# Differential cross-attention and a routed feed-forward layer on one core: a step of sixteen chunks laid out as eight slots of two chunks, with the side work of every engine in a new order

## The reference

```python
n = layernorm(x)
q, k, v = n @ Wq.T, ctx @ Wk.T, ctx @ Wv.T          # q, k: 32 sub-heads of 8; v: 16 heads of 16
att = softmax(q_j @ k_j.T / sqrt(8))                # 128 x 128 for each of 32 sub-heads
att = att[even] - lam * att[odd]                    # 16 heads
x = x + att @ v
h = layernorm(x)
shared = silu(h @ ws_gate) * (h @ ws_up) @ ws_down
w, e = top_k(sigmoid(h @ gate_w.T), 2); w = 2.5 * w / sum(w)
x = x + shared + sum_k w_k * (silu(h @ w_gate[e_k]) * (h @ w_up[e_k])) @ w_down[e_k]
```

## Time and profile before

| | |
|---|---|
| median of 3 runs | 2256.83 us (2256.3 to 2265.62) |
| the profiled execution, its own time | 2249.22 us |
| its span in the trace | 2247.5 us |
| PE busy | 2021.7 us, 90% of the span |
| DVE, ACT, POOL busy | 71%, 63%, 64% |
| mean granted TensorE clock | 0.972 of full speed |
| DMA | 432.05 MB, mean 192 GB/s |

### The profile page before, as it was taken

How to read it: one execution, slowest core, us unless ns; L and a number is a source line. 1 busy time by engine, 2 the same in 40 slices (tenths; PEclk the granted TensorE clock), 3 DMA queues, 4 the chain that set the end, 5 groups by cost and what they waited for, 6 DMA issues and landing times.

```text
span 2247.5 us, 76469 instructions
## 1 busy us (share of the span) xinstructions
PE 2021.7 (90%) x20840; PEld 1405.2 (63%) x20840; DVE 1584.5 (71%) x4623; ACT 1426.2 (63%) x3511; POOL 1446.2 (64%) x2183
## 2 busy tenths in 40 slices
PE   4999999999999999999999999999977988889996
PEld 3666665566656566656656566666546877768775
DVE  3777777777777777778777777778765655546554
ACT  2777777777777777777776777777763444434443
POOL 4466777767677676767676767767664555545554
PEclk8899999999999999999999999999987999999999
DMA  5997777777777777777777777878846777667774
GB/s 133 222 225 192 187 195 190 178 189 184 191 190 184 186 194 185 185 183 182 191 193 178 184 188 190 194 181 216 228 173 180 223 214 214 199 178 220 220 223 127
DMA packets 616921, 432.05 MB, mean 192 GB/s; under 512 B 447811, under 2 KB 562634, under 8 KB 616400
## 3 DMA queue, kind: packets, MB, share of 16 engines
q1 hardware_dynamic: 556528, 319.91, 58.3%
q0 software_dynamic: 32256, 84.47, 11.8%
q10 hardware_dynamic: 28000, 26.03, 3.8%
HBM read 234.59 MB, written 197.72 MB: 192 GB/s over the span
## 4 chain that ended last, share of the span: by engine, by line
PE 67%; DVE 15%; issue 10%; ACT 3%; DMA 2%; SPq 1%; POOL 1%; DVEq 1%; another core or an unknown queue 1%; ACTq 0%; POOLq 0%
PE mx_ps L494 11%; PE o_ps L527 7%; DVE mx L982 6%; PE ms_ps L778 5%; PE o_ps L538 5%; PE ms_ps L555 5%; PE mx_ps L557 4%; PE mx_ps L555 4%; PE ms_ps L576 4%; PE st_ps L756 3%; PE mx_ps L556 3%; PE ms_ps L583 3%; PE st_ps L487 3%; PE ms_ps L556 3%; PE ms_ps L557 2%
## 5 line engine op out<-in xcount | busy, mean ns | idle before, releaser
L982 DVE TENSOR_REDUCE mx<-mx_ps 128x4 f32<-128x512 f32 x1024 | 686.3, 685 | 300.4 <-PE mx_ps L494 294.2
L826 ACT ACTIVATE prob<-st_ps 128x512 f32<-128x512 f32 x1024 | 604.5, 598 | 357.8 <-PE st_ps L487 353.5
L494 PE MATMUL mx_ps<-stacks 48*128 48x128 bf16 x4096 | 396.7, 221 | 67.6 <-DVE mx L982 33.8
L487 PE MATMUL st_ps<-stacks 50*128 50x128 bf16 x4096 | 394.9, 220 | 0.0
L494 PEld LDWEIGHTS mx_ps<-stacks 48*128 48x128 bf16 x4096 | 230.9, 95 | 228.6 <-issue 105.9
L527 PE MATMUL o_ps<-prob,v_sb 128*32 128x256 f32 x4096 | 331.6, 396 | 0.8 <-ACT prob L826 0.4
L1344 POOL DMA_INDIRECT rows_dram<-rowt,posi x256 | 253.7, 991 | 67.6 <-issue 64.3
L555 PE MATMUL ms_ps<-e_lo 128*128 128x256 f32 x768 | 264.7, 345 | 18.1 <-issue 11.1
L923 ACT ACTIVATE rows_T<-st_ps 128x256 fp32r<-128x256 f32 x288 | 111.7, 388 | 192.2 <-PE st_ps L756 137.3
L487 PEld LDWEIGHTS st_ps<-stacks 50*128 50x128 bf16 x4096 | 229.8, 95 | 2.5 <-issue 1.5
L1413 POOL DMA_INDIRECT sums_dram<-stacks x144 | 141.7, 984 | 130.4 <-DVE stacks L1220 70.2
(11 more groups left out here) (155 smaller groups left out, 4694.4 us busy)
## 6 DMA issues: line engine op xcount, KB each, us to landing
stack_dram<-w_dn_sb SPq DMA_DIRECT2D x768, 128.0 KB
stacks<-stack_dram SPq DMA_DIRECT2D x512, 192.0 KB
stacks<-rows_dram SPq DMA_DIRECT2D x288, 130.0 KB
w_dn_sb<-in_x SPq DMA_DIRECT2D x64, 256.0 KB
w_dn_sb<-in_ctxT SPq DMA_DIRECT2D x64, 256.0 KB
x_res<-in_x SPq DMA_DIRECT2D x64, 256.0 KB
stacks<-sums_dram SPq DMA_DIRECT2D x78, 128.0 KB
stacks<-base_dram SPq DMA_DIRECT2D x76, 128.0 KB
```

The source lines that it names most:

```text
L487: return pe.matmul(st_ps[k % 2][:, i * P:(i + 1) * P], k_st[p][64 * h:64 * h + KROWS, u, j, :], q_st[p][64 * h:64 * h + KROWS, u, j, :], s ...
L494: return pe.matmul(mx_ps[k % 2][:, i * P:(i + 1) * P], q_st[p][64 * h:64 * h + ROWS, u, j, :], k_st[p][64 * h:64 * h + ROWS, u, j, :], sta ...
L826: nc.scalar.activation(prob[k % 4][:, :], st_ps[k % 2][:, :], ACT.Exp, scale=float(HALF) ** -0.5).then_inc(a_exp, 1)
L982: v.tensor_reduce(mx[:, u, c * CHUNK:(c + 1) * CHUNK], mx_ps[k % 2][:, :].rearrange("p (c n) -> p c n", c=CHUNK), AX.X, ALU.max).then_inc( ...
```

## The change

What it does, part by part:

- **Slots.** The loop over 16 chunks becomes one over 8 slots (`NSL`), each of two chunks. `st_ps` and `mx_ps` become one tensor over two banks each; one exponential and one reduction read 1024 columns. TensorE now waits, before it writes slot n, for the exponential and the reduction of slot n-1, since both banks are read by one instruction. `attend` of a slot comes a slot later. Semaphore counts follow.
- **Side jobs.** The two halves of `value` and of each projection are issued together; all side jobs have new slots; `gate_up` signals each half.
- **VectorE.** `shared_gate`/`shared_up` and `low`/`shared_add` stand ahead of the slot's reduction; `indices` is split off `best_two`. The arithmetic of `places` works on a copy `rank` in SBUF, which ScalarE makes by one more instruction of 128 columns a step, and TensorE's `clear` waits for this copy.
- **GpSimd.** The scatters of pair `r` move one step later (`r3 = it-3`); `split` of the queries moves to the next step, behind two scatters and a residual.
- **SyncE.** The twelve parts are issued together, after `put_max(it, 1)`; the four loads for the next step's first half stand together, then `put_max(b, 0)`.
- **The ends.** Two more steps are written out ahead of the loop, and the experts' weight splits at the stage's end keep nearly their places.

```diff
-            def both(it, b, k, do_c, do_b):
+            def both(it, b, n, do_c, do_b):
...
-                    wait(pe, v_red, NCH, b, k - 1)
+                    wait(pe, v_red, NSL, b, n)
...
-                for i in range(CHUNK):
+                for k in (2 * n, 2 * n + 1):
+                    for i in range(CHUNK):
...
-                        if it.is_in(0, NS + (1 if k < 2 else 0)):
-                            wait(pe, a_exp, NCH, it, k - 1)
-                    both(it, b, k, cur, b.is_in(0, NS))
+                        wait(pe, a_exp, NSL, it, n)
+                    both(it, b, n, cur, b.is_in(0, NS))
...
-                        nc.scalar.activation(prob[k % 4][:, :], st_ps[k % 2][:, :], ACT.Exp,
+                        nc.scalar.activation(prob_all[n % 2][:, :], st_all[:, :], ACT.Exp,
...
-                                mx_ps[k % 2][:, :].rearrange("p (c n) -> p c n", c=CHUNK), AX.X,
+                                mx_all[:, :].rearrange("p (c n) -> p c n", c=2 * CHUNK), AX.X,
...
+                if n == 0 and do_b:
+                    clear(it, "M0", 0)
+                    value(b, 0)
+                    value(b, 1).then_inc(p_v, 1)
+                if n == 0 and do_c:
+                    clear(it, "TO", 0)
+                    turn_max(it, 1)
...
+                if n == 5 and do_a:
+                    clear(it, "M1", 2)
+                    wait(pe, v_x, 1, a, 1)
+                    project(0, (x_hi, x_lo), M1, 0)
+                    project(0, (x_hi, x_lo), M1, 1).then_inc(p_q, 1)
+                if n == 5 and do_r:
+                    clear(it, "M0", 3)
+                    wait(pe, v_hot, 1, r, 1)
+                    ranks()
...
+                    if n == 6 and do_r:
+                        wait(act, p_pf, 1, r, 1)
+                        wait(act, v_pf, 1, r)
+                        nc.scalar.activation(rank[:, 0:4 * E2], M0[:, 0:4 * E2], ACT.Copy).then_inc(a_rank, 1)
...
+                if do_k:
+                    split(k2, q_rest, qp, a_qb, g_qs)
+                    split(k2, k_rest, kp, a_kb, g_ks)
```

More of the change, by code:

```diff
@@ L1113, in step @@
                     do_r = False
-                for k in range(NCH):
-                    if it.k is None and (it.off, k) in EARLY_LOW:
-                        expert_low(*EARLY_LOW[it.off, k])
+                for n in range(NSL):
+                    if it.k is None and (it.off, n) in EARLY_LOW:
+                        expert_low(*EARLY_LOW[it.off, n])
+                    if n == 5 and do_a:
+                        low(a, M1, a_x, x_hi, x_lo, v_x)
+                    if n == 5 and do_r:
+                        shared_add(r, M0)
+                    if n == 3 and do_r:
+                        shared_gate(r)
+                        shared_up(r)
```

464 lines of the change are left out of this document (216 added, 248 removed).

## The result

The changed kernel takes 2375.23 us (median of 4 runs) against 2258.78 for the kernel before on the same chip: ratio 1.050, 95% interval 1.046 to 1.054. It is slower by 116 us; I had forecast 2170. The profiled execution has 2375.2 us.

The account below looks back on a forecast made before the run. TensorE, 93% busy in attention steps, was taken as the bound: 22.26 us work plus 1.65 waits gives 23.91 against 25.27 a step, 87 us less over 64 steps. Forecast 2170 us, range 2095 to 2280.

Parts of the forecast that it names:

- TensorE's own time: Attention step: fewer turn-arounds cut TensorE's work from 23.57 to 22.26 us, a gain of at most 1.31.
- the joined slots: TensorE's pairs: seven of eight slots newly joined, each saving 0.11 us, 0.77 us a step.
- the joined projections' 0.54: Value, query and key projections on TensorE: three joins of halves save 0.18 us each, 0.54 a step.
- Reading instructions: VectorE and ScalarE: a 1024-column reduction takes 1.22 us, a double exponential 1.02; gains off the path, counted at nothing.
- What the lost alternation costs: TensorE waits for late VectorE results in slots 4, 5 and 0: together 1.65 us a step, at most 3.0.
- The cover of the bare slots: Next slot may begin at 1.93 us; shortest slots hold 2.3 us of TensorE work, covered by 0.3 at worst.
- slot 4: `turn_max` needs the bank `combine` reads; reduction at 0.65 us, so TensorE waits 0.45 us.
- Rival B: Attention step: waits of 3.0 us eat the gain, 25.27 us a step, 2257 us; chance 0.12 including gains below 0.5%.
- GpSimd and SyncE: Later query `split` delays SyncE's twelve parts; loads land by 22 us of a 23.9 us step, costing nothing.
- I count it at nothing: SyncE's loads land 2 us before the step ends; this cover costs zero, each us late would cost 64 us.
- rival C: SyncE's parts start too late, each step waits for first stacks until about 27 us: 2366 us; chance 0.14.
- The copy of the ranks: ScalarE's new 128-column copy, below 0.42 us, stands in a slot with over 0.5 us to spare: no cost.

Follow-up runs that it names:

- e12: Changed kernel, second norm in tiles of its own (its values left out of scattered rows), `key_rest` behind the first two scatters: ratio to before 1.025.
- e15: e12 with VectorE's `combine` ahead of the reduction in slots 0 and 4: ratio to before 1.003.
- e1: Kernel before with slots of two chunks alone, other engines' order as before: ratio to before 1.036.
- e6: Changed kernel with all four scatters first in GpSimd's step and `key_rest` behind them: ratio to before 1.100.
- e14: Changed kernel with only both `turn_max` moved one slot later: ratio to before 1.050.
- e9: Kernel before with only the halves of the value, query and key projections joined: ratio to before 1.014.
- c2: Control: the changed kernel itself on the chips where the kernel before takes 2064 us: ratio to before 1.098.
- e2: Changed kernel with four row buffers instead of two and the loop unrolled four times: ratio to before 1.065.
- e11: Changed kernel with the second norm written to tiles of its own, its values left out of the scattered rows: ratio to before 1.031.
- e16: Changed kernel with only `combine` put ahead of the reduction in slots 0 and 4: ratio to before 1.027.
- e10: Kernel before with only ScalarE's copy of the ranks to SBUF, where `places` then works: one run, 2249.85 us.
- e4: Changed kernel with `key_rest` behind GpSimd's first two scatters: ratio to before 1.058.
- e5: Changed kernel with `key_rest` writing zeros in place of its subtraction, those key values left out: ratio to before 1.040.

## Why the prediction was wrong

I forecast 23.91 us a step; by the measure of the table it is 27.32. Of the 3.4 us between them 0.7 are TensorE's work (22.99 for 22.26) and 2.7 its waits (4.33 for 1.65).

**TensorE's own time: right in kind, at the same clock, and above my bound.** I had 1.31 us less, and wrote that nothing lets it exceed that. e12 against the kernel before on sort II: 23.14 to 21.67, 1.47 less, at 1.00 of the clock before and 0.99 after; on sort I e15 has 21.76 against 23.72, 1.96 less. Eight pairs take 0.55 us as forecast. That e1 gives 0.75 for the joined slots against 0.77 is in part luck, since its clock is 0.98 against 1.00. The versions of the changed kernel on sort II do the same products in 23.39 us a step at 0.92 (e6) and 21.73 at 1.00 (e14), about 0.2 for each 0.01; by this estimate e1's clock hides 0.4, and the joined slots save some 1.2. Likewise the joined projections' 0.54 does not show in e9's time: its work falls by 0.06 at 0.96 against 0.99, and its waits grow by 0.51. What I left out: the changed kernel's granted clock is lower. Its stretches of 3 us around slot 0's wait at `turn_max`, which ends at 959.26:

```profile
954.00:957.00 3.00, 2.86 (x39) 2.11 (x38) 2.76 (x11) 2.65 (x6) 1.36 (x2) 1.00 0.98 216
957.00:960.00 3.00, 1.19 (x19) 0.94 (x20) 2.03 (x5) 1.25 (x4) 1.25 (x2) 0.93 0.31 46
960.00:963.00 3.00, 3.00 (x22) 1.85 (x17) 1.60 (x3) 1.72 (x3) 2.77 (x4) 0.50 0.28 94
963.00:966.00 3.00, 3.00 (x36) 2.03 (x34) 2.90 (x8) 2.08 (x5) 2.09 (x3) 1.00 0.53 116
```

TensorE is busy 1.19 of 3 us, and the next stretch is granted 0.50, the 1.2 GHz level. `gate_up`, which stands there, takes 466 ns a record in the changed kernel (L576; 439 in c2) and 393 in e12. On sort II the same products cost 22.82 us a step in the changed kernel and 21.67 in e12: 1.15 us, most of the 1.47 that the joining had won. The sum of the idle time does not tell the clock: e2 idles 3.57 us a step at 0.96, e15 3.58 at 1.00, e9 2.27 at 0.96. Which property of the waits does was not tested.

**Reading instructions: right.** 1221 ns for the reduction of 1024 columns (I had 1.22), 1.02 us for the exponential (1.02).

**What the lost alternation costs: right in kind, too small.** The cover of the bare slots held (0.34 us a step at the pairs). `turn_max` and `ranks` are where TensorE waits. But even with the ring cut the idle time is 2.74 us, not 1.65: 1.6 at `turn_max`, 0.5 at `hot`, and 0.5 for the maxima's rows, a wait for a DMA that I had excluded. In slot 4 I started the reduction 0.65 us after the pairs; in e12's step at 906.89 it starts after 1.19, since VectorE's statistics stand ahead and wait 0.70 for GpSimd's residual:

```profile
907.33 0.43 DVE L1004 BATCH_NORM_STATS2 bs<-x 128x6 f32<-128x256 f32 x1 [0.70 <-POOL x L1328]
...
908.08 1.23 DVE L967 TENSOR_REDUCE mx<-mx_ps 128x8 f32<-128x1024 f32 x1
...
910.08 0.22 PE L544 MATMUL o_ps<-identb,mxp 128*64 128x128 bf16 x1 [0.93 <-DVE o_sc L988]
```

`hot`, for which I had allowed about 0.75 with the indices, takes 0.4 in e12 and 0.69 in the changed kernel, rather than 0.22, since `context_low` holds it. Rival B's price, 3.0 us, was nearer than mine. The Trainium skill's rule on rotating banks ("Perfetto Trace Analysis", section Optimizing Tensor Performance) agrees with e1 alone: where the layout of the side jobs stays, 1.4 us a step appear as waiting for the reduction.

**GpSimd and SyncE: the step that failed.** "I count it at nothing." I followed the queries' parts to their landing and found 2 us of cover. That part was sound: SyncE's twelve parts take 6.90 us from 908.70, its loads start at 917.58, and TensorE waits for `stacks` in the changed kernel by 1.2 us in 1400. So rival C's mechanism is false, and that its 2366 us is near the measured 2375 is luck. What I did not follow is who else waits for what was moved: the four scatters. Their landing releases ScalarE's norm, and the move by one step took a step's slack out of a ring that passes every engine. On sort II: the ring costs 2.34 us (e11), or 2.54 with the key's rest out of the way (e12), 1.39 of it idle time of TensorE and 1.15 longer work at the lower clock. What is left of e12, 0.59 above the kernel before, is 2.06 of further waits, for VectorE and for the maxima's rows, less 1.47 of joining. On sort I, where the forecast was made, the ring was not cut by itself. There the changed step is 1.84 us longer than before; `combine` first takes 0.78 out of it (e16), and the ring cut with the key's rest late another 1.20 (e15).

**The copy of the ranks.** I priced ScalarE's 128 columns and never the operations that now read SBUF. They cost the step nothing alone (e10). Taking `key_rest` from beside them gives 1.43 us in the closed ring, where e4 also lets the scatters go earlier, and 0.20 in the open one.

## What to carry to other kernels

- When a transfer is moved by a step, list every wait on its semaphore and count how many steps lie between issue and wait, before and after. Slack that falls from one step to none closes a ring, and then time on any link, on whatever engine, can be time of the step.
- Edits that each win a us in such a ring don't add up, and one that helps while it is closed can cost once it is cut (`turn_max`: 1.82 gained, 0.25 lost). Cut the ring first, then tune.
- On an engine that is 93% busy, new waits can cost twice: by their length, and by the slower clock of the work behind them. Read the granted clock of each version before its busy time is compared with another's.

## What the runs showed of the hardware

A VectorE instruction of 64 columns with both inputs in SBUF took up to 1.22 us beside a 1.16 us reading instruction of GpSimd, and in most cases 0.22 beside an issue of scatters (e10: 229 ns in the mean) or a GpSimd write of zeros (e5: 218; one of two such lines 298). A loop unrolled four times showed some 11 stops of TensorE of up to 4.9 us in 1300 us, about one in four or five steps; unrolled twice, no such stop stands out. That this is the loop's turn is argued from the count, not shown. Chips differ: the same kernel before took 2259 or 2064 us, with the second stage's DMA at 206 against 248 GB/s (2000 to 2240 us and 1800 to 2000) and its attention step at 25.48 against 23.82 us, both at 0.99 to 1.00 of the clock; why the step differs stays open.
